# A two-layer state-space block over 8 cores: the output projection of a chunk is written out after the next chunk's loads, the scan's y sum gets a PSUM tensor of its own, and the delta stage moves from the head of a block to its fourth pair

## The reference

```python
xz = einsum('bld,ed->ble', rmsnorm(x, w), in_w)     # 1024 -> 4096
xb, z = split(xz)
xb = silu(causal_conv4(xb) + cb)
dbc = einsum('ble,re->blr', xb, xp_w)               # 2048 -> 64 + 16 + 16
delta = softplus(dbc[..., :64] @ dtw.T + dtb)
dA = exp(delta[..., None] * -exp(a_log))
mi = delta[..., None] * Bm[:, :, None, :] * xb[..., None]
def scan_fn((h, v), (dA_t, mi_t, C_t)):
    v = 0.6 * v + mi_t
    h = dA_t * h + v
    return (h, v), einsum('ben,bn->be', h, C_t)
y = (scan + dp * xb) * silu(z)
x = x + einsum('ble,de->bld', y, ow)                # 2048 -> 1024
```

## Time and profile before

| what | us |
|---|---|
| median of 3 runs | 26583.62 (26580.75 to 26587.31) |
| the profiled execution, its own time | 26579.49 |
| its span on core 3, the slowest | 26577.7 |
| the spans of the 8 cores | 26462.5 to 26577.7 |
| DVE busy | 17561.2 (66% of the span) |
| POOL busy | 9645.7 (36%) |
| ACT busy | 6224.1 (23%) |
| PE busy (matmul) | 5587.0 (21%) |

### The profile page before, as it was taken

One profiled execution on the slowest core, in us unless ns is written; L12 is line 12 of the kernel. 1 busy time (PEld: TensorE's weight loads), 2 busy tenths in 40 slices (PEclk: granted clock), 3 DMA queues, 4 the chain that ended last, 5 costly groups with the idle time before them and its releaser, 6 DMA issues.

```text
span 26577.7 us, 149004 instructions; the slowest of 8 cores (26462.5 to 26577.7 us)
## 1 busy us (share of the span) xinstructions
PE 5587.0 (21%) x27585; PEld 2809.8 (11%) x27585; DVE 17561.2 (66%) x35295; ACT 6224.1 (23%) x12996; POOL 9645.7 (36%) x13524
## 2 busy tenths in 40 slices
PE   1121111212222112221211122222221112121345
PEld 0010000101111001110100011111110001010033
DVE  2677766777777777774777766777777766765222
ACT  1222222222222222221222222222222222221111
POOL 4334333333334433335344333333334433334000
PEclk7555555555555555555555555555555555555677
DMA  3000000000000000002000000000000000002211
GB/s 27 8 6 5 6 9 8 8 8 8 8 7 6 5 7 8 8 8 28 7 7 4 9 8 8 8 8 8 8 6 8 4 8 9 8 8 37 62 40 44
DMA packets 587345, 327.23 MB, mean 12 GB/s; under 512 B 228416, under 2 KB 586272, under 8 KB 586400
## 3 DMA queue, kind: packets, MB, share of 16 engines
q10 hardware_dynamic: 179712, 88.16, 3.6%
q1 hardware_dynamic: 233120, 186.16, 2.3%
q0 software_dynamic: 173568, 43.38, 1.8%
HBM read 292.92 MB, written 67.80 MB: 14 GB/s over the span
## 4 chain that ended last, share of the span: by engine, by line
DVE 59%; PE 9%; issue 9%; DMA 9%; ACTq 5%; ACT 4%; POOL 2%; SPq 1%; DVEq 1%; POOLq 0%
DVE hg L553 22%; DVE vg L539 19%; DVE hcl L571 6%; ACTq L433 5%; PE pmm L353 4%; DVE vg L548 3%; DVE vcar L561 2%; DVE hcar L564 2%; DMA bmc<-bcrows 2%; DVE tmpb L401 1%; DVE tmpa L401 1%; PE pout L579 1%; DMA wa_out<-xfm 1%; DVEq L978 1%; POOL wa_in L240 1%
## 5 line engine op out<-in xcount | busy, mean ns | idle before, releaser
L520 POOL TENSOR_TENSOR mig<-ubf,bmc 128x256 bf16<-128x256 bf16 x4096 | 2759.3, 674 | 13547.5 <-DVE vg L539 7623.1
L553 DVE TENSOR_TENSOR_SCAN hg<-dag,hcar,vg 128x514 bf16<-128x514 f32 x4096 | 5687.1, 1388 | 713.1 <-DVE vg L548 659.4
L579 PE MATMUL pout<-hcl,identb 128*128 128x256 bf16 x8192 | 2483.5, 400 | 15689.4 <-DVE hcl L571 15689.4
L528 POOL TENSOR_TENSOR mig<-ubf,bmc 128x256 bf16<-128x256 bf16 x4096 | 5370.6, 1311 | 596.7 <-POOL mig L520 14.7
L539 DVE TENSOR_TENSOR_SCAN vg<-beta,vcar,mig 128x514 bf16<-128x514 f32 x4096 | 5240.5, 1279 | 284.0 <-POOL mig L533 283.4
L502 ACT ACTIVATE dag<-dfl,nega 128x256 f32<-128x256 f32 x4096 | 2069.1, 505 | 9247.2 <-DVE hg L553 9247.2
L579 PEld LDWEIGHTS pout<-hcl,identb 128*128 128x128 bf16 x8192 | 848.2, 104 | 17318.8 <-DVE hcl L571 13059.8
L513 ACT ACTIVATE dag<-dfl,nega 128x256 f32<-128x256 f32 x4096 | 2084.7, 509 | 133.9
L571 DVE TENSOR_TENSOR hcl<-hg,bmc 128x256 bf16<-128x256 bf16 x8192 | 1983.8, 281 | 0.0
L561 DVE COPY vcar<-vg 128x2 bf16<-128x2 bf16 x4096 | 1714.8, 419 | 140.6
L473 DVE TENSOR_TENSOR dfl<-spa,spb 128x256 f32<-128x256 f32 x512 | 217.6, 425 | 2323.4 <-ACT spb L471 2323.4
(11 more groups left out here) (110 smaller groups left out, 7503.6 us busy)
## 6 DMA issues: line engine op xcount, KB each, us to landing
bmc<-bcrows ACTq DMA_DIRECT2D x1024, 64.0 KB, 15.3
wa_in<-w_in POOLq DMA_DIRECT2D x512, 32.0 KB, 2.7
xf<-xfm SPq DMA_DIRECT2D x128, 128.0 KB
xre<-xfm SPq DMA_DIRECT2D x128, 128.0 KB
xresA<-xre SPq DMA_DIRECT2D x128, 128.0 KB
xf<-xresA SPq DMA_DIRECT2D x128, 128.0 KB
xre<-xresA SPq DMA_DIRECT2D x128, 128.0 KB
xresB<-xre SPq DMA_DIRECT2D x128, 128.0 KB
```

Of the source, the lines that this page charges most:

```text
L520: e.tensor_tensor(mig[:, go:go + T], ubf[:, dslot:dslot + T], bmc[:, n0 * T:(n0 + 1) * T], Alu.mult),
L528: e.tensor_tensor(mig[:, go + T + 1:go + 2 * T + 1], ubf[:, dslot:dslot + T], bmc[:, n1 * T:(n1 + 1) * T], Alu.mult),
L553: e.tensor_tensor_scan(hg[:, go:go + GW], dag[:, go:go + GW], vg[:, go:go + GW], hcar[:, j * 16 + n0:j * 16 + n0 + 1], Alu.mult, Alu.add),
L579: e.matmul(pout[:, yslot:yslot + T], identb[:], hcl[:, hc_o:hc_o + T], start=(n == 0), stop=(n == 15)),
```

## The change

Three edits.

1. The y sums of the scan go to a new PSUM tensor `pyy`, and `pout` is left to the output projection, whose matmuls no longer wait for the `yfl` reads of the block before.
2. The output projection of chunk c (its loads, matmuls, additions and stores) is wrapped in a function and recorded in chunk c+1, behind the 8 `xf` loads and ahead of the squares. That of the last chunk of a layer is recorded behind the loop.
3. `stage_dt(j + 1)` is recorded in block j ahead of pair g = 3, not ahead of pair g = 0.

```diff
+    pyy = pst("pyy", [128, 1024])
...
+            if pending_backend is not None:
+                pending_backend()
             t_st = []
             t_sq_l = [None] * 8
...
             for j in range(16):
                 dslot = (j % 2) * T
                 yslot = (j % 2) * 512
-                if j + 1 < 16:
-                    stage_dt(j + 1)
...
                 for g in range(8):
+                    if g == 3 and j + 1 < 16:
+                        stage_dt(j + 1)
                     n0 = 2 * g
...
-                                           pout[:, yslot:yslot + T], identb[:],
+                                           pyy[:, yslot:yslot + T], identb[:],
...
-                    pout[:, yslot:yslot + T], Alu.mult, Alu.add), [t_ymm[15]])
+                    pyy[:, yslot:yslot + T], Alu.mult, Alu.add), [t_ymm[15]])
...
-            for dt_i in range(8):
...
-                        [t_y[15] if (dt_i == 0 and j == 0) else None,
-                         t_y2_slot_c[dt_i % 2] if j == 0 else None,
-                         (t_ev[dt_i - 2] if dt_i >= 2 else t_outevac_prev)
-                         if j == 0 else None])
...
+            def mk_backend(c=c, co=co, t_y15=t_y[15], ys_snap=tuple(t_y2_slot)):
+                def backend():
+                    t_om = None
+                    t_ev = [None] * 8
+                    for dt_i in range(8):
...
+                                [t_y15 if (dt_i == 0 and j == 0) else None,
+                                 (t_ev[dt_i - 2] if dt_i >= 2 else BST["oev"])
+                                 if j == 0 else None])
...
+                return backend
+            pending_backend = mk_backend()
+        if pending_backend is not None:
+            pending_backend()
```

More of the change, by code:

```diff
@@ L277, in mamba_layer @@
         t_evac31_prev = None
-        t_outevac_prev = None
-        t_outmm_prev = None
-        t_xre_guard = None
+        BST = {"oev": None, "omm": None, "xre": None}
+        pending_backend = None
         t_bmc_cons_v = None
@@ L604, in mamba_layer @@
                     Alu.mult),
-                    [t_y2, t_evac[16 + j], t_outmm_prev if j == 0 else None, DBGB()])
+                    [t_y2, t_evac[16 + j], BST["omm"] if j == 0 else None, DBGB()])
                 if dbg and l == 0 and c == 0:
@@ L616, in mamba_layer @@
             t_sp_last_prev = t_sp4
-            t_ev = [None] * 8
-            t_om = None
-            for dt_i in range(8):
[L621 to L631, removed]
-                        [t_y[15] if (dt_i == 0 and j == 0) else None,
-                         t_y2_slot_c[dt_i % 2] if j == 0 else None,
-                         (t_ev[dt_i - 2] if dt_i >= 2 else t_outevac_prev)
-                         if j == 0 else None])
[L636 to L641, removed]
-                                            e.dma_start(
-                    out=dst_ap[dt_i * 128:(dt_i + 1) * 128, co:co + T],
-                    in_=xre[:, ro:ro + T]), [t_ev[dt_i]])
@@ L645, in mamba_layer @@
[L645 to L649, removed]
+            def mk_backend(c=c, co=co, t_y15=t_y[15], ys_snap=tuple(t_y2_slot)):
[3 more added lines that the diff above has]
+                    for dt_i in range(8):
+                        po = (dt_i % 2) * 512
+                        ro = (dt_i % 2) * T
+                        t_xr = wdma("sync", lambda e, dt_i=dt_i, co=co, ro=ro: e.dma_start(
+                            out=xre[:, ro:ro + T],
+                            in_=src_ap[dt_i * 128:(dt_i + 1) * 128, co:co + T]),
+                            [t_ev[dt_i - 2] if dt_i >= 2 else BST["xre"]])
+                        for j in range(16):
+                            t_om = wop("tensor", lambda e, j=j, dt_i=dt_i, po=po: e.matmul(
+                                pout[:, po:po + T],
+                                wa_out[:, (j * 8 + dt_i) * 128:(j * 8 + dt_i + 1) * 128],
+                                ybl[:, j * T:(j + 1) * T], start=(j == 0), stop=(j == 15)),
+                                [t_y15 if (dt_i == 0 and j == 0) else None,
+                                 (t_ev[dt_i - 2] if dt_i >= 2 else BST["oev"])
+                                 if j == 0 else None])
+                        t_ev[dt_i] = wop("vector", lambda e, dt_i=dt_i, po=po, ro=ro:
+                                         e.scalar_tensor_tensor(
+                                             xre[:, ro:ro + T], pout[:, po:po + T],
+                                             1.0, xre[:, ro:ro + T],
+                                             Alu.mult, Alu.add),
+                                         [t_om, t_xr])
+                        dst_store[c] = wdma("sync", lambda e, dt_i=dt_i, co=co, ro=ro:
+                                            e.dma_start(
+                            out=dst_ap[dt_i * 128:(dt_i + 1) * 128, co:co + T],
+                            in_=xre[:, ro:ro + T]), [t_ev[dt_i]])
+                    BST["xre"] = t_ev[7]
+                    BST["oev"] = t_ev[7]
+                    BST["omm"] = t_om
+                return backend
@@ L651, in build_program @@
+            pending_backend = mk_backend()
+        if pending_backend is not None:
+            pending_backend()
+        return dst_store, t_sp_last_prev, t_inproj_last, BST["omm"], t_xp_last
     storeA, t_spA, t_li, t_lo, t_lx = mamba_layer(0, xfm, xresA, t_wl0, None)
```

## The result

| kernel | median, us | lowest to highest | runs |
|---|---|---|---|
| before | 26585.47 | 26569.14 to 26601.31 | 8 |
| changed | 27178.62 | 27124.23 to 27216.12 | 8 |

The ratio is 1.0221 with a 95% interval of 1.021 to 1.0232: 593 us slower. The forecast was 27156, 572 us slower. The profile after is that of core 5, with a span of 27180.3 us; that of before was core 3.

A forecast was written before the change was run, and what follows sets the result against it. The prediction took DVE as the scan's pacemaker. Stage +848, late projection -321, delayed rows +45 and PSUM tensor 0 took the span from 26577.7 to 27149.7, hence a time of 27156 us, range 27070 to 27300.

The forecast's parts named there:

- The chain keeps its length and loses its cover: Delta stage at pair 3: `dfl` still 3.34 us behind `hcl`, without `yfl` and `ybl` between; DVE waits 2.86, not 1.25.
- 15 insertions at 3.82, 14 boundaries at 2.20, nothing back for block 1: +848 us: Scan, per chunk: 57.3 us paid at pair 3, 30.8 saved at block boundaries; net 26.5 us, times 32 chunks.
- The squares start 1.9 us behind the last addition; -321 us: Chunk changes: early `xf` loads leave the path, gaining 16.5 us in layer 1 and 4.9 in layer 0, 15 times each.
- The rows held up: +45 us: Chunk front: early `xf` loads run beside the `bmc` loads of B and C rows and delay them, ends 0 and 189.
- 1.5 us a chunk: Delay of the B and C rows by early loads, picked between 0 and 6.3 us; 30 times gives +45 us.
- the 3.8 us of work: DMA work of the 8 `xf` loads: 61% busy over their 6.3 us stretch.
- the 114 us: Alternative to the 45: queues taking turns push all `xf` work into a full `bmc` queue, 30 x 3.8; sum 27225.
- The PSUM tensor: 0: Output projection: separate y sums remove only a wait for `yfl` already covered by that for the last `ybl`; 0 us.
- The sum, 572: Whole kernel: stage, late projection and delayed rows together make it 572 us slower, 27156 us, 2.2%.

The follow-up runs named there:

- e4: Changed kernel with only the delta stage's matmul recorded one pair earlier, ahead of pair 2, the rest staying at pair 3: 25772.89 us, ratio 0.9704.
- e1: Kernel before with only the delta stage of block j+1 moved ahead of pair 3: 27423.39 us, ratio 1.0325.
- e5: Changed kernel with the delta stage ahead of pair 5 in place of pair 3: 27205.32 us, ratio 1.0228.
- e2: Changed kernel with the delta stage back at the head of the block, leaving the PSUM tensor and late output projection: 26372.32 us, ratio 0.9927.
- e3: As e2, with the next chunk's xf loads made to wait for the 32 loads of B and C rows: 26264.91 us, ratio 0.9891.
- e8: Changed kernel with the stage's matmul one pair earlier and the xf loads waiting for the B and C rows: 25706.36 us, ratio 0.967.
- e7: Kernel before with only the y sums in their own PSUM tensor and no projection wait for yfl: 26577.13 us, ratio 0.9993.
- e6: As e8, with yfl and ybl of a block recorded behind pair 0 of the next block: 25799.59 us, ratio 0.9703.

## Why the prediction was right

- **The chain keeps its length and loses its cover.** This is the step on which everything hung, and it is shown. The step from `hcl` to `dfl` is 3.34 us in the earlier trace rows and after, the wait 2.86 as stated, and e4 takes it all away by moving the one instruction that was named.
- **15 insertions at 3.82, 14 boundaries at 2.20, nothing back for block 1: +848 us.** e1 measured +849, and the scan's stretch in the table grew by 843 us, 26.3 a chunk where 26.5 were worked out. e5 shows that pair 5 is no better than pair 3.
- **The squares start 1.9 us behind the last addition; -321 us.** The trace has 1.88, the table gives -325 and the waits of e2 give 333. e3, which has no cost beside the gain, measured -309.
- **The rows held up: +45 us.** This term was too small. The tails say 84 in the changed kernel and 72 in e2; the gate gave back 107 us (e3) and about 90 (e8), or 79 and 81 by the mean spans. A part of the 84 is scatter: e1 and e7, whose loads stand where they did before, have layer 0 tails of 67.9 and 68.0 us, and the kernel before 66.6. Over all chunks the four profiles with the loads beside the rows (changed, e2, e4, e5) have 2040 to 2066 us of tail, and before, e1, e3 and e7 have 1977 to 1998; the means lie 64 us apart. That puts the term between 64 and 107 us, within its range of 0 to 189. The error did not matter because the term is small beside the others.

The reason for picking 1.5 us a chunk does not hold either. It read the engines' busy share of 0.57 as room. In other chunks of the same core and layer, before, the share is anything from 0.25 to 0.74 at almost the same rate. The rows are of the windows view, core 3, 2 to 54 us behind the `bcrows` store; columns as in the earlier trace rows.

```profile
18443.39:18495.39 52.00, 0.39 (x1) 0.10 (x1) 1.70 (x4) 6.66 (x13) 0.11 (x1) 0.50 0.25 43
...
22885.44:22937.44 52.00, 0.39 (x1) 0.10 (x1) 1.70 (x4) 6.66 (x13) 0.00 (x0) 0.50 0.74 42
```

So the share of one chunk says little about how much more the queue can take, and the 3.8 us of work that a share of 0.61 gave, and the 114 us made from them, rest on the same kind of reading. The rule of the Trainium skill on the turns between queues (DMA: Bandwidth & Descriptors, Queues, rings and completion order) was used for those 114 us. That is near the 107 of e3 and above the 79 and 81 of the mean spans, and no run here shows the turns themselves. That the loads are slowed beside the rows is seen in their 59.74 us, and that the rows are, in the tails.

- **The PSUM tensor: 0.** e7 agrees within its interval.
- **The sum, 572.** Measured 593, and 606 by the mean spans of the two profiles. The table divides the 606: the two large terms are within 5 us of the forecast, and the term for the rows is 45 short.

e1 and e2 add up to 849 - 202 = +647 us and the whole change measured +593. By the mean spans the three are +857, -244 and +598 (27117.6 for the changed kernel, against the first group's before), so the sum is +613 and the gap 15 us. The scan's stretch is the same in e1 and in the changed kernel, 18814 us, and so is the step to the first square in e2 and there, 57 us; the two edits show no effect on each other, and most of the gap of 54 us lies in which core was slowest.

Left open: why e8 and e6, with the gate and the earlier matmul, have layer 0 tails of 65.1 and 64.7 us, less than the kernel before, and why the tails of layer 0 are so long in its first chunks.

## What to carry to other kernels

A stage that crosses engines is as late as its first instruction's place in that engine's list: before moving it, ask what stands ahead of it there. To hide it, move its first link up by more than the chain's length and leave the last link where it is; here one pair, 3.98 us from `hcl` to `hcl` in e8, was enough for a chain of 3.34. Taking a stage out of a boundary also takes it out from beside the work that covered part of it, so count the wait at the new place, not the old one. When two variants differ by less than the cores of one run do, compare the mean span of all cores, and cut the timelines into stretches. A prefetch needs a free path as well as free time: let it start behind the transfers that someone waits for.

## What the runs showed of the hardware that was not expected

- Eight loads of 128 KB, each waiting for the one before, took 15.54 us from first to last issue with no other load of the core beside them, and 59.74 beside 32 loads of 64 KB that spread one row over 128 partitions. The other way round, the time from the store of the rows to the first v scan grew by 1.0 us beside them, and by 4.6 in the layer where the eight are in flight together (1.2 and 3.1 between the means of the four profiles with them and the four without).
- The busy share of the DMA engines was 0.25 in one chunk and 0.74 in another, with the same loads at 43 and 42 GB/s.
- The front's 289 matmuls took 51.39 us in a chunk of e2 at a granted clock of 0.64, and 44.31 in the same chunk of e3 at 0.75; the stretch took 82.40 and 75.60.
- Removing a wait of 0.50 us on DVE lengthened the operations of DVE and POOL around it by more than the wait (e6): 242 us of DVE's waits went, and 338 of busy time came.
